# A head reordered: squares before copies, masks and keys on another engine, both bias halves in a row

## The chip, the core and the metric

The kernel runs on one core of a Trainium2 chip. Five engines work side by side, each through its own queue in order: TensorE (PE, matmuls and transposes), VectorE (DVE), ScalarE (ACT), GpSimd (POOL) and SyncE (SP, which here only issues DMAs). They wait for one another by semaphores. The metric is the device time of one launch in microseconds (us); lower is better.

## What is computed

Four images of 64 channels and 32x32 positions go through a local attention with windows of 7x7 (`conv`) and then through a token model whose steps are chosen by the data (`ffn`). The head of the kernel is the channel norm, the query fold and the position biases of the local attention:

```python
def _ln_c(v, eps=1e-06):
    m = jnp.mean(v, axis=1, keepdims=True)
    s = jnp.var(v, axis=1, keepdims=True)
    return (v - m) / jnp.sqrt(s + eps)
...
    q, k, v = (jnp.einsum('oc,bchw->bohw', w, xp) for w in (wq, wk, wv))   # xp: padded norm
    bias_x = jnp.einsum('bgxhw,xk->bhwk', qx, rel_x)       # qx, qy: halves of each group of q
    bias_y = jnp.einsum('bgyhw,yk->bhwk', qy, rel_y)
    logits = jnp.einsum('bchw,bchwkl->bhwkl', win_q, win_k)
    logits = logits + bias_x[:, :, :, None, :] + bias_y[:, :, :, :, None]
    attn = softmax(logits over the 49 window places)
    out = jnp.einsum('bhwkl,bchwkl->bchw', attn, win_v)
...
x = x + _L0_conv_ref(_ln_c(x), ...)
t = tokens(x);  t = t + _L0_ffn_ref(_ln_t(t), ...)
```

## The kernel before, in words

Two images lie on 128 partitions (64 channels each), so there are two image pairs, and each pair has 1024 positions in two chunks of 512: chunks 0 and 1 are "image 0" of the change's name, chunks 2 and 3 are "image 1". Each engine's program is written out by hand; its order is the order of the code, and nothing rearranges it.

The head runs from the loads to `scores(0)`. For each chunk j:

- TensorE: `centre(j)` (L346) subtracts the channel mean by a matmul into PSUM bank j.
- ScalarE: `square(0, j)` squares it into `sq` (L789) and copies it out to `xc` (L791).
- TensorE: `variance(0, j)` (L356) averages the squares with weights of 32 columns, four matmuls.
- ScalarE: `root(0, j)` (L806) takes the square root of variance plus epsilon.
- VectorE: `inverse(0, j)` (L1089) is its reciprocal.
- TensorE: `spread(0, j)` (L369) spreads it over the channels, four matmuls; it takes the whole width of the array.
- VectorE: `scale(0, j)` (L1106) multiplies `xc` by it into the padded image `h_pad` and raises `normed`.

Beside this chain TensorE turns the key weights and folds them with the query weights (`tables`, L387 and L389, and `fold_keys`, L396); ScalarE copies the results (`wk_nat` L820, `tabs` L825, `wqk_bd` L827). `queries(0)` (L404) makes the queries of chunk 0. `biases(a, half)` (L425, L428) makes half of the position biases of image pair a in 32 small matmuls, each 32 columns wide in the array. For each half, `add_bias` on VectorE (L1124, L1129) adds the masks and writes two operands of the scores. ScalarE writes the masks (L836, four copies of 32 rows, broadcast) and the keys' one-hot rows (L840, two instructions).

A matmul of float32 shows as two records in the trace: centre is x2, variance and spread are x8.

`scores(0)` (L471, L476) waits for the keys, the query copy and all four add_bias instructions. Then a loop over 16 pairs of blocks follows (scores, maxima, exponentials, normalise, transposes, mix), then the token model. Three more biases and later norms of the second kind use the same helpers in the loop.

Which PSUM bank holds what is set by tables: `QBANK` (queries), `BBANK` (biases), `CENTRE_AT`, `VAR_AT`, `SPREAD_AT`. The tables of `tables` and `fold_keys` lie in bank 7.

Of the kernel before, what the change touches and what calls it, by code (L numbers as in the profile page):

```python
# [25 lines left out]
ALU = mybir.AluOpType  # L26
# [3 lines left out]
P = 128  # L30
# [18 lines left out]
SCALE = float(C) ** -0.5  # L49
LN_C_EPS, LN_T_EPS = 1e-6, 1e-5  # L50
GBANK = (2, 6, 6, 6)
QBANK, VBANK, BBANK = (0, 7, 7, 7), (6, 7, 7, 7), (2, 3, 7, 7)
W2COLS = 2 * C + 2 + 1
TWICE = ((0, 0), (1, 0), (0, 1), (1, 1))
RING = 15
# [6 lines left out]
def build(nc, x, w_qk, w_q, w_v, bias_tables, key_onehot, masks, ident, mean_mat, spread_mat, iotas,  # L62
          attn_mask, ffn_mask, attn_pack, ffn_w1, ffn_pack, out):
    with ExitStack() as ctx:
# [278 lines left out]
        def _(pe):  # L343
            def centre(j, bank=None):

                nc.tensor.matmul(ps[:, j if bank is None else bank, :], centre_w[:], x2f[:, j * 512:j * 512 + 512],  # L346
                                 start=True, stop=True).then_inc(S["centred"], 1)

            def variance(k, j):

                bank, at = VAR_AT[k][j]
                pe.wait_ge(S["squared"], 4 * k + j + 1)
                if k == 0 and j >= 2:
                    pe.wait_ge(S["normed"], j - 1)
                for s in range(4):
                    mm = nc.tensor.matmul(ps[32 * s:32 * s + 32, bank, at:at + P], mean_w[:, P:P + 32],  # L356
                                          sq[:, j * 512 + P * s:j * 512 + P * s + P], start=True, stop=True)
                mm.then_inc(S["var_ready"], 1)

            def spread(k, j):  # L360

                banks, at = SPREAD_AT[k][j]
                if k == 1 and j < 3:
                    pe.wait_ge(S["rooted"], 1)
                else:
                    pe.wait_ge(S["inv_ready"], 5 if k else j + 1)
                for odd in range(2):
                    for r in range(2):
                        mm = nc.tensor.matmul(ps[:, banks[r], at + P * odd:at + P * odd + P],  # L369
                                              spread_w[C * r:C * r + C, odd, :],  # L370
                                              sq[C * r:C * r + C, j * 512:j * 512 + P], start=True, stop=True)
                mm.then_inc(S["spread_ready"], 1)
# [10 lines left out]
            def tables():  # L383

                pe.wait_ge(S["t_loaded"], 48)
                pe.wait_ge(S["eye_loaded"], 16)
                nc.tensor.transpose(ps[0:C, 5, 0:C], wqk[:, C:P], eye[0:C, 0:C]).then_inc(S["wk_turned"], 1)  # L387
                for h in range(2):
                    nc.tensor.matmul(ps[C * h:C * h + C, 7, 0:TX + TY], wq_nat[:], rel_tab[:],  # L389
                                     start=True, stop=True)  # L390

            def fold_keys():

                pe.wait_ge(S["wk_copied"], 1)
                for h in range(2):
                    mm = nc.tensor.matmul(ps[C * h:C * h + C, 7, P:P + C], wq_nat[:], wk_nat[:],  # L396
                                          start=True, stop=True)
                mm.then_inc(S["tab_ready"], 1)

# [35 lines left out]
            pe.wait_ge(S["x0_loaded"], 32)  # L435
            centre(0)
            centre(1)
            tables()
            variance(0, 0)
            fold_keys()  # L440
            pe.wait_ge(S["x1_loaded"], 32)
            centre(2)
            variance(0, 1)
            pe.wait_ge(S["s_loaded"], 64)
            spread(0, 0)
            pe.wait_ge(S["tab_copied"], 4)
            spread(0, 1)
            centre(3)
            variance(0, 2)
            pe.wait_ge(S["centre_copied"], 1)  # L450
            queries(0)
            pe.wait_ge(S["centre_copied"], 3)
            biases(0, 0)
            variance(0, 3)
            spread(0, 2)
            pe.wait_ge(S["centre_copied"], 4)
            biases(0, 1)
            spread(0, 3)

            def turn_row(bank, src=h2):  # L460
# [3 lines left out]
            def scores(p):  # L464

                a, hb, xb = p // 8, p % 8 // 2, p % 2
                blk = 4 * xb + hb
                if p >= 2:
                    pe.wait_ge(S["exp_done"], p - 1)
                for h in range(2):  # L470
                    nc.tensor.matmul(ps[:, 2 * xb + h, 0:NKEY], q_blk[C * h:C * h + C, a, blk, :],  # L471
                                     h_pad[C * h:C * h + C, a, BR * hb:BR * hb + KR, BC * xb:BC * xb + KC],
                                     start=True, stop=False)
                for part in range(2):
                    for h in range(2):
                        mm = nc.tensor.matmul(ps[:, 2 * xb + h, 0:NKEY], b_st[C * h:C * h + C, part, a, blk, :],  # L476
                                              k_st[C * h:C * h + C, part], start=False, stop=(part == 1))
                mm.then_inc(S["scores_ready"], 1)
# [38 lines left out]
            pe.wait_ge(S["q_copied"], 1)  # L517
            pe.wait_ge(S["bias_added"], 4)
            scores(0)
            scores(1)  # L520
            pe.wait_ge(S["w_loaded"], 32)
            pe.wait_ge(S["normed"], 4)
# [258 lines left out]
        def _(act):  # L781
# [2 lines left out]
                nc.scalar.activation(spare[:, 0:1], eps_c[:, 0:1], func)  # L784

            def square(k, j):
                bank = CENTRE_AT[k][j]
                act.wait_ge(S["centred"], 4 * k + j + 1)
                nc.scalar.activation(sq[:, j * 512:j * 512 + 512], ps[:, bank, :],  # L789
                                     ACT.Square).then_inc(S["squared"], 1)  # L790
                nc.scalar.copy(xc[:, j * 512:j * 512 + 512], ps[:, bank, :]).then_inc(S["centre_copied"], 1)  # L791

            def copy_variance(j):
                act.wait_ge(S["var_ready"], 4 + j + 1)
# [8 lines left out]
            def root(k, j):  # L803
                bank, at = VAR_AT[k][j]
                act.wait_ge(S["var_ready"], 4 * k + j + 1)
                nc.scalar.activation(sq[:, j * 512:j * 512 + P], ps[:, bank, at:at + P], ACT.Sqrt,  # L806
                                     bias=eps_c[:, k:k + 1]).then_inc(S["std_ready"], 1)
# [7 lines left out]
            act.wait_ge(S["eps_set"], 1)  # L815
            load_table(ACT.Sqrt)
            square(0, 0)
            act.wait_ge(S["w_zeroed"], 1)
            act.wait_ge(S["wk_turned"], 1)
            nc.scalar.copy(wk_nat[:], ps[0:C, 5, 0:C]).then_inc(S["wk_copied"], 1)  # L820
            square(0, 1)
            root(0, 0)
            act.wait_ge(S["tab_ready"], 1)
            for h in range(2):
                nc.scalar.copy(tabs[C * h:C * h + C, h, :], ps[C * h:C * h + C, 7, 0:TX + TY]  # L825
                               ).then_inc(S["tab_copied"], 1)
                nc.scalar.copy(wqk_bd[C * h:C * h + C, C * h:C * h + C], ps[C * h:C * h + C, 7, P:P + C]  # L827
                               ).then_inc(S["tab_copied"], 1)
            square(0, 2)
            root(0, 1)  # L830
            act.wait_ge(S["c_loaded"], 64)
            for h in range(2):
                for y in range(2):
                    rows = slice(C * h + 32 * y, C * h + 32 * y + 32)
                    src = masks_in[rows, 0:BR].unsqueeze(2) if y else masks_in[rows, 0:BC].unsqueeze(1)
                    nc.scalar.copy(masks_xy[rows, :].rearrange("p (r c) -> p r c", c=BC),  # L836
                                   src.broadcast_to([32, BR, BC])).then_inc(S["masks_set"], 1)
            act.wait_ge(S["k_loaded"], 32)
            for part in range(2):
                nc.scalar.mul(k_st[:, part], onehot[:, :, 0:KC], 1.0 - 2 * part).then_inc(S["keys_set"], 1)  # L840
            square(0, 3)
            root(0, 2)
            root(0, 3)
            load_table(ACT.Exp)

# [56 lines left out]
            for p in range(1, NPAIR - 2):  # L902
                copy_turned(p)
                copy_values(p + 1)
                if p in (3, 6):
                    copy_queries(2 + p // 6)
                if p in (4, 5):
                    copy_projected(p - 2)
                if p in (8, 10, 12):
                    square(1, p // 2 - 4)  # L910
                if p in (9, 11, 13):
                    copy_variance((p - 9) // 2)
                if p == 9:
                    load_next()
                exps(p + 2)
# [3 lines left out]
            root_three()  # L919
            copy_turned(15)  # L920
            square(1, 3)
            root(1, 3)
            load_table(ACT.Exp)

# [117 lines left out]
        def _(dve):  # L1042
# [71 lines left out]
            dve.wait_ge(S["pads_set"], 1)  # L1114
            scale(0, 0)
            scale(0, 1)
            inverse(0, 2)

            def add_bias(a, half):

# [9 lines left out]
                    b_map[:, 1, a, :, :, cols], b_top[:, 0, a, :, :, cols], -1e29, raw,  # L1130
                    ALU.max, ALU.subtract).then_inc(S["bias_added"], 1)

            dve.wait_ge(S["masks_set"], 4)
            add_bias(0, 0)
            inverse(0, 3)
            scale(0, 2)
            add_bias(0, 1)
            scale(0, 3)

            def maxima(p):  # L1140
# [292 lines left out]
```

## Time and profile before

| | us |
|---|---|
| median of 3 runs | 242.87 (242.84 to 243.87) |
| span of the profiled execution | 240.6 |
| TensorE matmul busy | 223.1 (93%) |
| VectorE busy | 157.0 (65%) |
| ScalarE busy | 158.3 (66%) |
| GpSimd busy | 26.2 (11%) |

The page gives the profiled execution's span, from its first instruction to its last, and no other time for it; the median of the runs is 2.27 above the span. Busy time is a sum over stages, and a busy TensorE is not one at its peak. What a change in the head is worth is read from the chain of waits and from the timelines of the engines in the first 24 us. A row of a timeline gives the start, the length from the first start to the last end of the instructions merged in it, and in brackets how long the engine was idle before it and what ended that.

### The profile page before, as it was taken

To read this page: it belongs to the slowest core of one execution; us is meant where nothing else is said; L and a number is where in the kernel's file an instruction comes from. 1 tells how busy PE (TensorE), PEld (TensorE's weight loads), DVE (VectorE), ACT (ScalarE), POOL (GpSimd) and SP (SyncE) were. 2 spreads that over 40 slices of the span, in tenths; PEclk is the share of its full clock that TensorE was granted. 3 is DMA by queue.
4 is the path that set the end of the run, shared out by engine and by line. 5 is a ranking of instruction groups with operands and counts; after the bars stand their busy time and mean duration, and the time that the engine had idled before them with its cause. 6 is when DMAs were issued, how large, how long until landed. Compare 5 with 4: busy or idle time off the path is not lost.

```text
span 240.6 us, 5412 instructions
## 1 busy us (share of the span) xinstructions
PE 223.1 (93%) x1995; PEld 153.9 (64%) x1996; DVE 157.0 (65%) x288; ACT 158.3 (66%) x310; POOL 26.2 (11%) x37
## 2 busy tenths in 40 slices
PE   7978989999899988999999999999999999998991
PEld 3347667666676665433576777888888888885320
DVE  1147636676866663664769999897679778753642
ACT  2573653476778784654579978789877777772641
POOL 9600231111212106200000000000000000000000
PEclk9999999999999999999999999999999999999998
DMA  6600000000010000000100000000000000000016
GB/s 141 149 0 5 0 1 4 3 0 0 4 33 3 1 3 0 0 4 11 34 0 4 0 3 0 3 1 3 0 3 0 3 0 1 3 3 0 0 29 147
DMA packets 3151, 3.60 MB, mean 15 GB/s; under 512 B 1077, under 2 KB 2229, under 8 KB 3126
## 3 DMA queue, kind: packets, MB, share of 16 engines
q1 hardware_dynamic: 2486, 2.59, 4.9%
q10 hardware_dynamic: 544, 0.66, 1.1%
q8 instruction: 16, 0.26, 0.4%
q14 instruction: 9, 0.07, 0.1%
q0 software_dynamic: 96, 0.00, 0.0%
HBM read 2.21 MB, written 1.05 MB: 14 GB/s over the span
## 4 chain that ended last, share of the span: by engine, by line
PE 74%; ACT 11%; DVE 9%; issue 5%; DVEq 0%; ACTq 0%
PE ps L681 12%; PE ps L667 11%; PE ps L646 11%; PE ps L734 6%; PE ps L748 6%; PE ps L509 4%; PE ps L497 3%; PE ps L471 3%; PE ps L381 3%; DVE negmax L1143 2%; ACT prob L866 2%; PE ps L346 2%; PE ps L627 1%; PE ps L425 1%; PE ps L486 1%
## 5 line engine op out<-in xcount | busy, mean ns | idle before, releaser
L1001 ACT COPY arena<-ps 128x1024 f32<-128x1024 f32 x32 | 32.4, 1012 | 15.8 <-PE ps L667 15.7
L646 PE MATMUL ps<-h_st,g_st 128*128 128x512 f32 x128 | 38.7, 424 | 0.7 <-ACT late L949 0.4
L1240 DVE TENSOR_REDUCE negmax<-ps 128x1 f32<-128x1024 f32 x32 | 38.4, 1217 | 1.4 <-PE ps L646 1.3
L949 ACT ACTIVATE late<-ps,negmax 128x1024 f32<-128x1024 f32 x32 | 35.9, 1122 | 5.0 <-DVE negmax L1240 4.4
L667 PE MATMUL ps<-eye,late 128*128 128x128 f32 x256 | 33.5, 274 | 0.6 <-DVE late L1250 0.2
L667 PEld LDWEIGHTS ps<-eye,late 128*128 128x128 f32 x256 | 29.1, 140 | 6.9 <-DVE late L1250 2.7
L681 PE MATMUL ps<-arena,late 128*64 128x128 f32 x512 | 31.5, 276 | 1.1 <-ACT arena L1001 1.1
L866 ACT ACTIVATE prob<-ps,negmax 128x308 f32<-128x308 f32 x32 | 16.4, 517 | 22.4 <-DVE negmax L1143 22.4
L681 PEld LDWEIGHTS ps<-arena,late 128*64 128x64 f32 x512 | 27.6, 137 | 3.8 <-issue 2.2
L646 PEld LDWEIGHTS ps<-h_st,g_st 128*128 128x128 f32 x128 | 21.8, 188 | 8.9 <-issue 3.2
L1250 DVE TENSOR_SCALAR late<-late,rinv 128x1024 f32<-128x1024 f32 x32 | 24.1, 754 | 1.1
L325 POOL TENSOR_TENSOR v_st<-arena,ones_c 128x308 f32<-128x308 f32 x16 | 11.9, 747 | 59.2 <-PE ps L486 37.9
L509 PE MATMUL ps<-prob_t,v_key 103*64 103x128 f32 x192 | 14.0, 281 | 4.5 <-ACT arena L856 1.1
L1143 DVE TENSOR_REDUCE negmax<-ps 128x2 f32<-128x616 f32 x16 | 12.7, 796 | 6.9 <-PE ps L476 6.9
L1016 ACT ACTIVATE arena<-ps,w2p 128x512 f32<-128x512 f32 x16 | 11.0, 690 | 7.1 <-PE ps L734 7.1
L734 PE MATMUL ps<-h,w1d 64*128 64x512 f32 x64 | 15.5, 614 | 0.0
L1152 DVE TENSOR_SCALAR prob<-prob,rinv 128x308 f32<-128x308 f32 x32 | 14.9, 507 | 0.6
L509 PEld LDWEIGHTS ps<-prob_t,v_key 103*64 103x64 f32 x192 | 10.2, 136 | 7.8 <-ACT arena L856 1.7
L748 PE MATMUL ps<-arena,w2p 128*64 128x512 f32 x64 | 15.1, 602 | 0.0
L877 ACT COPY prob_t<-ps 103x384 f32<-103x384 f32 x32 | 13.7, 485 | 1.6 <-PE ps L497 1.4
L497 PE MATMUL ps<-eye,prob 128*103 128x128 f32 x96 | 14.4, 286 | 0.2 <-DVE prob L1152 0.2
L1247 DVE RECIPROCAL rinv<-rowsum 128x1 f32<-128x1 f32 x32 | 5.1, 161 | 13.2 <-ACT late L949 12.3
(125 smaller groups left out, 317.7 us busy)
## 6 DMA issues: line engine op xcount, KB each, us to landing
out<-osum SPq DMA_DIRECT2D x8, 128.0 KB, 2.4
x<-in_x SPq DMA_DIRECT2D x2, 256.0 KB, 5.4
x<-in_x ACTq DMA_DIRECT2D x2, 256.0 KB, 5.9
onehot<-in_key_onehot SPq DMA_DIRECT2D x2, 133.0 KB, 2.8
w1d<-in_ffn_w SPq DMA_DIRECT2D x4, 64.0 KB, 2.2
w2p<-in_ffn_pack SPq DMA_DIRECT2D x2, 65.5 KB, 2.1
spread_w<-in_spread_mat SPq DMA_DIRECT2D x4, 32.0 KB, 5.8
mean_w<-in_mean_mat SPq DMA_DIRECT2D x1, 96.0 KB, 2.3
```

The costliest lines, as they stand in the source:

```text
L497: mm = nc.tensor.transpose(ps[0:CH, 4 + h, c * P:c * P + P], prob[:, pp, h, c * CH:c * CH + CH], eye[:])
L509: mm = nc.tensor.matmul(ps[C * h:C * h + C, 7, 0:P], v_key[0:CH, pp, c, C * h:C * h + C], prob_t[0:CH, pp, h, c, :], start=(c == 0), stop= ...
L646: mm = nc.tensor.matmul(ps[:, 2 * h + c, :], g_st[:, b2, h, q0:q0 + P], h_st[:, b2, h, part, c * 512:c * 512 + 512], start=(part == 0), st ...
L667: mm = nc.tensor.transpose(ps[:, bank + i, (c % 4) * P:(c % 4) * P + P], pr[:, n % 2, c * P:c * P + P], eye[:])
L681: mm = nc.tensor.matmul(ps[C * h:C * h + C, 7, cols], vk[:, g // 2, c, C * h:C * h + C], prt[:, g % 2, h, c, cols], start=(c == 0), stop=( ...
L734: mm = nc.tensor.matmul(ps[:, set0 + 2 * h + c, :], w1d[C * h:C * h + C, c * P:c * P + P], h2[C * h:C * h + C, t * 512:t * 512 + 512], sta ...
L748: mm = nc.tensor.matmul(ps[C * h:C * h + C, set0 + bank, :], w2p[:, c * C:c * C + C], hid[t % 2][:, 2 * h + c, :], start=(i == 0), stop=(i ...
L866: ins = nc.scalar.activation(prob[:, pp, h, 0:NKEY], ps[:, 2 * pp + h, 0:NKEY], ACT.Exp, bias=negmax[:, pp, h:h + 1], accum_out=rowsum[:, ...
L949: nc.scalar.activation(pr[:, n % 2, :], ps[:, 2 * (n % 2):2 * (n % 2) + 2, :], ACT.Exp, bias=negmax[:, 0, n % 2:n % 2 + 1], accum_out=rows ...
L1001: nc.scalar.copy(prt[:, n // 8 % 2, n % 2, :, q0:q0 + P], ps[:, bank:bank + 2, :].rearrange("p b (c q) -> p (b c) q", c=4)).then_inc(S["s_ ...
L1240: nc.vector.tensor_reduce(negmax[:, 0, n % 2:n % 2 + 1], ps[:, 2 * (n % 2):2 * (n % 2) + 2, :], mybir.AxisListType.XY, ALU.max, negate=Tru ...
L1250: nc.vector.tensor_scalar(pr[:, n % 2, :], pr[:, n % 2, :], rinv[:, 0, n % 2:n % 2 + 1], None, ALU.mult).then_inc(S["s_prob"], 1)
```

## The change

Four things are changed in the head, and the banks that go with them:

1. ScalarE's `square` is split into `square` and `copy_centred`. In the head both squares of image pair 0 stand ahead of their copies, the roots go between, and TensorE's `variance(0, 0)` and `variance(0, 1)` stand ahead of `tables` and `fold_keys`. The same split in the later loop keeps the order.
2. The masks and the keys are written by VectorE instead of ScalarE, behind `scale(0, 1)`.
3. TensorE centres chunk 3 and takes both variances of image pair 1 ahead of the biases; VectorE takes both its reciprocals ahead of the first `add_bias`.
4. Both bias halves stand in a row on TensorE, `queries(0)` and the two spreads of image pair 1 behind them; both `add_bias` stand in a row on VectorE, the two scales behind them.

The tables move to bank 3, the biases to banks 0 and 1, the first queries to bank 2. The wait for `tab_copied` now stands ahead of `centre(3)`, and `scores(1)` gets a wait for the last copy.

```diff
-QBANK, VBANK, BBANK = (0, 7, 7, 7), (6, 7, 7, 7), (2, 3, 7, 7)
+QBANK, VBANK, BBANK = (2, 7, 7, 7), (6, 7, 7, 7), (0, 1, 7, 7)
...
-                    nc.tensor.matmul(ps[C * h:C * h + C, 7, 0:TX + TY], wq_nat[:], rel_tab[:],
+                    nc.tensor.matmul(ps[C * h:C * h + C, 3, 0:TX + TY], wq_nat[:], rel_tab[:],
...
             centre(1)
+            variance(0, 0)
             tables()
-            variance(0, 0)
+            variance(0, 1)
             fold_keys()
             pe.wait_ge(S["x1_loaded"], 32)
             centre(2)
-            variance(0, 1)
             pe.wait_ge(S["s_loaded"], 64)
             spread(0, 0)
+            spread(0, 1)
             pe.wait_ge(S["tab_copied"], 4)
-            spread(0, 1)
             centre(3)
             variance(0, 2)
-            pe.wait_ge(S["centre_copied"], 1)
+            variance(0, 3)
+            biases(0, 0)
+            biases(0, 1)
+            pe.wait_ge(S["centre_copied"], 3)
             queries(0)
-            pe.wait_ge(S["centre_copied"], 3)
-            biases(0, 0)
-            variance(0, 3)
             spread(0, 2)
-            pe.wait_ge(S["centre_copied"], 4)
-            biases(0, 1)
             spread(0, 3)
...
             scores(0)
+            pe.wait_ge(S["centre_copied"], 4)
             scores(1)
...
             square(0, 0)
+            square(0, 1)
+            root(0, 0)
             act.wait_ge(S["w_zeroed"], 1)
             act.wait_ge(S["wk_turned"], 1)
             nc.scalar.copy(wk_nat[:], ps[0:C, 5, 0:C]).then_inc(S["wk_copied"], 1)
-            square(0, 1)
-            root(0, 0)
+            copy_centred(0, 0)
+            root(0, 1)
+            copy_centred(0, 1)
...
             square(0, 2)
-            root(0, 1)
-            act.wait_ge(S["c_loaded"], 64)
...
-                    nc.scalar.copy(masks_xy[rows, :].rearrange("p (r c) -> p r c", c=BC),
...
-            act.wait_ge(S["k_loaded"], 32)
...
-                nc.scalar.mul(k_st[:, part], onehot[:, :, 0:KC], 1.0 - 2 * part).then_inc(S["keys_set"], 1)
+            copy_centred(0, 2)
             square(0, 3)
             root(0, 2)
+            copy_centred(0, 3)
             root(0, 3)
...
             scale(0, 0)
             scale(0, 1)
-            inverse(0, 2)
...
+            dve.wait_ge(S["c_loaded"], 64)
+            for h in range(2):
+                for y in range(2):
+                    rows = slice(C * h + 32 * y, C * h + 32 * y + 32)
+                    src = masks_in[rows, 0:BR].unsqueeze(2) if y else masks_in[rows, 0:BC].unsqueeze(1)
+                    nc.vector.tensor_copy(masks_xy[rows, :].rearrange("p (r c) -> p r c", c=BC),
+                                          src.broadcast_to([32, BR, BC])).then_inc(S["masks_set"], 1)
+            dve.wait_ge(S["k_loaded"], 32)
+            for part in range(2):
+                nc.vector.tensor_scalar(k_st[:, part], onehot[:, :, 0:KC], 1.0 - 2 * part, None, ALU.mult
+                                        ).then_inc(S["keys_set"], 1)
+            inverse(0, 2)
+            inverse(0, 3)
             dve.wait_ge(S["masks_set"], 4)
             add_bias(0, 0)
-            inverse(0, 3)
+            add_bias(0, 1)
             scale(0, 2)
-            add_bias(0, 1)
             scale(0, 3)
```

ScalarE before, from the first copy of a chunk to the root of chunk 1 (the last row; ps is PSUM, sq the squares and later the roots, xc the centred chunk):

```order
L791 COPY xc<-ps 128x512
L820 COPY wk_nat<-ps 64x64 [waits wk_turned,w_zeroed]
L789 ACTIVATE sq<-ps 128x512 [waits centred]
L791 COPY xc<-ps 128x512
L806 ACTIVATE sq<-ps,eps_c 128x128 [waits var_ready]
L825 COPY tabs<-ps 64x98 [waits tab_ready]
L827 COPY wqk_bd<-ps 64x64
L825 COPY tabs<-ps 64x98
L827 COPY wqk_bd<-ps 64x64
L789 ACTIVATE sq<-ps 128x512 [waits centred]
L791 COPY xc<-ps 128x512
L806 ACTIVATE sq<-ps,eps_c 128x128 [waits var_ready]
```

ScalarE in the changed kernel, from the squares of chunks 0 and 1 (the first row is both) to the table copies:

```order
L787 ACTIVATE sq<-ps 128x512 [waits centred] x2
L808 ACTIVATE sq<-ps,eps_c 128x128 [waits var_ready]
L824 COPY wk_nat<-ps 64x64 [waits wk_turned,w_zeroed]
L792 COPY xc<-ps 128x512 [waits centred]
L808 ACTIVATE sq<-ps,eps_c 128x128 [waits var_ready]
L792 COPY xc<-ps 128x512 [waits centred]
L830 COPY tabs<-ps 64x98 [waits tab_ready]
L832 COPY wqk_bd<-ps 64x64
```

The root of chunk 1 has moved from behind four table copies, a square and three chunk copies to behind one chunk copy.

VectorE before, from the scale of chunk 1 to that of chunk 3 (h_st holds the scores' bias operands and the keys, late holds the padded image):

```order
L1106 TENSOR_TENSOR late<-xc,ps 128x16x32 [waits spread_ready,centre_copied]
L1089 RECIPROCAL sq<-sq 128x128 [waits std_ready]
L1124 TENSOR_TENSOR h_st<-ps,masks_xy 128x64x8 [waits bias_ready,masks_set]
L1129 SCALAR_TENSOR_TENSOR h_st<-h_st,ps 128x64x8 [waits bias_added]
L1089 RECIPROCAL sq<-sq 128x128 [waits std_ready]
L1106 TENSOR_TENSOR late<-xc,ps 128x16x32 [waits spread_ready,centre_copied]
L1124 TENSOR_TENSOR h_st<-ps,masks_xy 128x64x8 [waits bias_ready]
L1129 SCALAR_TENSOR_TENSOR h_st<-h_st,ps 128x64x8 [waits bias_added]
L1106 TENSOR_TENSOR late<-xc,ps 128x16x32 [waits spread_ready,centre_copied]
```

VectorE in the changed kernel, the same stretch:

```order
L1104 TENSOR_TENSOR late<-xc,ps 128x16x32 [waits spread_ready,centre_copied]
L1135 COPY masks_xy<-masks_in 32x128 [waits c_loaded]
L1135 COPY masks_xy<-masks_in 32x128 x3
L1139 TENSOR_SCALAR h_st<-onehot 128x308 [waits k_loaded]
L1139 TENSOR_SCALAR h_st<-onehot 128x308
L1087 RECIPROCAL sq<-sq 128x128 [waits std_ready] x2
L1121 TENSOR_TENSOR h_st<-ps,masks_xy 128x64x8 [waits bias_ready,masks_set]
L1126 SCALAR_TENSOR_TENSOR h_st<-h_st,ps 128x64x8 [waits bias_added]
L1121 TENSOR_TENSOR h_st<-ps,masks_xy 128x64x8 [waits bias_ready]
L1126 SCALAR_TENSOR_TENSOR h_st<-h_st,ps 128x64x8 [waits bias_added]
L1104 TENSOR_TENSOR late<-xc,ps 128x16x32 [waits spread_ready,centre_copied] x2
```

Six mask and key instructions have come in, and both add_bias now stand behind both reciprocals and ahead of both scales.

## Rows read from the trace of the kernel before

**Rows 1.** The page, part 4: the chain that ended last, by engine.

```profile
PE 74%; ACT 11%; DVE 9%; issue 5%; DVEq 0%; ACTq 0%
```

**Rows 2.** The chain of waits, 8 to 24 us: start, us, what.

```profile
13.07 0.96 DVE sq L1089
...
14.17 0.71 PE ps L369 x8
...
19.51 0.70 DVE h_st L1124
...
22.33 0.68 DVE h_st L1124
...
23.03 0.70 DVE h_st L1129
```

**Rows 3.** Timeline of ScalarE, 8 to 15 us: start, us, engine, line, operation.

```profile
8.46 0.60 ACT L789 ACTIVATE sq<-ps 128x512 f32<-128x512 f32 x1 [2.33 <-PE ps L346]
8.96 0.58 ACT L791 COPY xc<-ps 128x512 f32<-128x512 f32 x1
...
10.96 0.23 ACT L825 COPY tabs<-ps 64x98 f32<-64x98 f32 x1
...
11.70 0.60 ACT L789 ACTIVATE sq<-ps 128x512 f32<-128x512 f32 x1
...
12.65 0.39 ACT L806 ACTIVATE sq<-ps,eps_c 128x128 f32<-128x128 f32 x1
12.92 1.24 ACT L836 COPY masks_xy<-masks_in 32x128 f32<-32x128 f32 x4
14.18 0.82 ACT L840 ACTIVATE h_st<-onehot 128x308 fp32r<-128x308 f32 x2
```

**Rows 4.** Timeline of TensorE, 7 to 11 us.

```profile
7.40 1.88 PE L346 MATMUL ps<-x,centre_w 128*128 128x512 f32 x4
...
9.29 0.24 PE L387 MATMUL ps<-eye,wqk 64*64 64x64 f32 x1
...
9.78 0.43 PE L356 MATMUL ps<-sq,mean_w 128*32 128x128 f32 x8
...
10.13 0.33 PE L396 MATMUL ps<-wk_nat,wq_nat 64*64 64x64 f32 x4
...
10.40 1.12 PE L346 MATMUL ps<-x,centre_w 128*128 128x512 f32 x2
```

**Rows 5.** Timeline of TensorE, 14 to 24 us; of each bias block the first row.

```profile
14.82 1.12 PE L346 MATMUL ps<-x,centre_w 128*128 128x512 f32 x2
15.87 0.43 PE L356 MATMUL ps<-sq,mean_w 128*32 128x128 f32 x8
16.23 1.16 PE L404 MATMUL ps<-late,wqk_bd 128*128 128x512 f32 x2
17.32 0.28 PE L425 MATMUL ps<-late,tabs 128*32 128x64 f32 x1
...
20.17 0.29 PE L425 MATMUL ps<-late,tabs 128*32 128x64 f32 x1
...
22.14 0.71 PE L369 MATMUL ps<-sq,spread_w 64*128 64x128 f32 x8
23.86 0.76 PE L471 MATMUL ps<-late,arena 64*128 64x308 f32 x3 [1.00 <-DVE h_st L1129]
```

**Rows 6.** VectorE: a group of instructions (busy, mean ns), and timelines at 27 and 64 us.

```profile
L1152 DVE TENSOR_SCALAR prob<-prob,rinv 128x308 f32<-128x308 f32 x32 | 14.9, 507 | 0.6
...
27.22 0.67 DVE L1152 TENSOR_SCALAR prob<-prob,rinv 128x308 f32<-128x308 f32 x2
...
64.31 0.28 DVE L1204 COPY twice_w<-eye 64x64 f32<-64x64 f32 x2
...
64.41 0.38 DVE L1204 COPY twice_w<-eye 64x64 f32<-64x64 f32 x2
```

**Rows 7.** Busy time in 13 to 14 us: PE, PEld, DVE, ACT, POOL, granted clock, DMA.

```profile
13.00:14.00 1.00, 0.00 (x0) 0.00 (x0) 0.93 (x2) 0.93 (x5) 0.00 (x0) 1.00 0.00 0
```

More of the change, by code:

```diff
@@ L395, in fold_keys @@
                 for h in range(2):
-                    mm = nc.tensor.matmul(ps[C * h:C * h + C, 7, P:P + C], wq_nat[:], wk_nat[:],
+                    mm = nc.tensor.matmul(ps[C * h:C * h + C, 3, P:P + C], wq_nat[:], wk_nat[:],
                                           start=True, stop=True)
@@ L786, in square, with copy_centred @@
             def square(k, j):
-                bank = CENTRE_AT[k][j]
                 act.wait_ge(S["centred"], 4 * k + j + 1)
-                nc.scalar.activation(sq[:, j * 512:j * 512 + 512], ps[:, bank, :],
+                nc.scalar.activation(sq[:, j * 512:j * 512 + 512], ps[:, CENTRE_AT[k][j], :],
                                      ACT.Square).then_inc(S["squared"], 1)
-                nc.scalar.copy(xc[:, j * 512:j * 512 + 512], ps[:, bank, :]).then_inc(S["centre_copied"], 1)
+            def copy_centred(k, j):
+                act.wait_ge(S["centred"], 4 * k + j + 1)
+                nc.scalar.copy(xc[:, j * 512:j * 512 + 512], ps[:, CENTRE_AT[k][j], :]
+                               ).then_inc(S["centre_copied"], 1)
             def copy_variance(j):
@@ L820, in _ @@
             nc.scalar.copy(wk_nat[:], ps[0:C, 5, 0:C]).then_inc(S["wk_copied"], 1)
-            square(0, 1)
-            root(0, 0)
+            copy_centred(0, 0)
+            root(0, 1)
+            copy_centred(0, 1)
             act.wait_ge(S["tab_ready"], 1)
             for h in range(2):
-                nc.scalar.copy(tabs[C * h:C * h + C, h, :], ps[C * h:C * h + C, 7, 0:TX + TY]
+                nc.scalar.copy(tabs[C * h:C * h + C, h, :], ps[C * h:C * h + C, 3, 0:TX + TY]
                                ).then_inc(S["tab_copied"], 1)
-                nc.scalar.copy(wqk_bd[C * h:C * h + C, C * h:C * h + C], ps[C * h:C * h + C, 7, P:P + C]
+                nc.scalar.copy(wqk_bd[C * h:C * h + C, C * h:C * h + C], ps[C * h:C * h + C, 3, P:P + C]
                                ).then_inc(S["tab_copied"], 1)
             square(0, 2)
-            root(0, 1)
-            act.wait_ge(S["c_loaded"], 64)
[L832 to L835, printed above, removed]
-                    nc.scalar.copy(masks_xy[rows, :].rearrange("p (r c) -> p r c", c=BC),
-                                   src.broadcast_to([32, BR, BC])).then_inc(S["masks_set"], 1)
-            act.wait_ge(S["k_loaded"], 32)
-            for part in range(2):
-                nc.scalar.mul(k_st[:, part], onehot[:, :, 0:KC], 1.0 - 2 * part).then_inc(S["keys_set"], 1)
+            copy_centred(0, 2)
             square(0, 3)
             root(0, 2)
+            copy_centred(0, 3)
             root(0, 3)
@@ L910, in _ @@
                     square(1, p // 2 - 4)
+                    copy_centred(1, p // 2 - 4)
                 if p in (9, 11, 13):
@@ L921, in _ @@
             square(1, 3)
+            copy_centred(1, 3)
             root(1, 3)
```

## The prediction

> **What bounds the kernel now.** I read the page's chain of waits first: most of the span is TensorE [rows 1], so the program is one long chain and there is no slack at its end for work that starts late. The change touches the first 24 us alone, so I then followed the chain from 8 us to the first scores. Three things are to be seen there. First, ScalarE copies chunks (xc, the first at 8.96) that nobody needs yet, and its roots stand behind: the root of chunk 1 starts at 12.65 [rows 3]. So VectorE's reciprocal of chunk 1 starts only at 13.07, TensorE is idle until its spread at 14.17, and centre(3) starts at 14.82 [rows 2, 5]. Second, from there TensorE works without a break through centre(3), a variance, queries(0), the two halves of the bias and the rest, until 22.8 or so [rows 5]. Third, VectorE ends the head: reciprocal and scale stand ahead of the second add_bias, whose two instructions run from 22.33 to 23.73, and scores(0) starts at 23.86 after 1.00 us of idle TensorE [rows 2, 5]. After that the loop over pairs has the same instructions in the same order in both kernels, and all its waits are on work of its own; the last DMA of the head (onehot) has long been used [rows 3]. So what scores(0) gains, the end gains. **The price of the change is the start of scores(0), against 23.86.**
>
> **Part 1: roots ahead of copies (image pair 0).** I walk the new order with the durations of now; a "slot" is the distance to the next start on the same engine. square(0,0) starts at 8.46 as now; a square or a copy has a slot of 0.50 (8.46 to 8.96) [rows 3]. centre(1) ends at 9.28 [rows 4], so square(0,1) runs 9.32 to 9.92. variance(0,0), now ahead of the tables, starts when centre(1) hands over, where the tables start now (9.29), and lasts 0.43 [rows 4]: 9.30 to 9.73. So root(0,0) takes ScalarE's next slot at 9.82 and its 0.39 ends at about 10.2 [rows 3]; the reciprocal (0.96) runs 10.23 to 11.18 [rows 2]. TensorE meanwhile does the tables from 9.66 (slot 0.49, from 9.29 to 9.78) and variance(0,1) from 10.15 to 10.58 [rows 4]. ScalarE does the small copy wk_nat at 10.10 (0.1 to 0.2) and one xc copy (0.50), and starts root(0,1) at 10.71, where it now starts at 12.65 [rows 3]. The second reciprocal then runs 11.12 to 12.07 instead of from 13.07 [rows 2].
>
> That is 1.95 us earlier, but TensorE cannot use it all: fold_keys at 10.51 (0.27), centre(2) at 10.78 (slot 1.05, as 14.82 to 15.87), spread(0,0) at 11.83 and spread(0,1) at 12.48 (slot 0.65, as 14.17 to 14.82) put centre(3) at 13.13 [rows 2, 4, 5]. The two spreads no longer wait. **Gain so far 14.82 - 13.13 = 1.69 us.** The wait of centre(3) for tab_copied is new (the tables now lie in bank 3, which centre(3) overwrites): ScalarE has one xc copy and the four table copies (10.96 to 11.70 now, 0.74) behind root(0,1), so it is done at 12.3 and the wait is covered by 0.9 [rows 3].
>
> **Part 2: both bias halves in a row.** From centre(3) TensorE has: centre(3) 1.05; variance(0,2) 0.36 (15.87 to 16.23), whose square is long done; a wait for square(0,3), since centre(3) ends at 14.25, the square 0.60 later, and variance(0,3) starts at 14.97: 0.43 of idle; variance(0,3) 0.36; two bias blocks; queries(0) 1.09 (16.23 to 17.32); two spreads, 0.65 each [rows 3, 5]. One block lasts 1.97 up to an instruction that takes the whole array (20.17 to 22.14), which includes a wait for a reciprocal; the sequence 17.32 to 20.17 less a variance (0.36) and a spread (0.65) leaves 1.84 for the other [rows 5]. I take 3.7 for the two, with 3.5 to 3.9 for the range. Sum 1.05 + 0.36 + 0.43 + 0.36 + 3.7 + 1.09 + 1.30 = 8.29; now it is 23.86 - 14.82 = 9.04. **Gain of this part 0.75 us**: the 1.00 of idle ahead of scores(0) goes, and about 0.4 of new wait comes. scores(0) would start at 13.13 + 8.29 = 21.42, if VectorE and ScalarE are ready by then.
>
> **Part 3: masks and keys on VectorE.** This takes 1.24 + 0.82 us from ScalarE [rows 3]. It is needed there: ScalarE is done with chunk 2 at about 13.2, and with 2.06 more it would come to square(0,3) at 15.3, not at 14.29, which Part 2 takes; those 1.0 us are in its sum. On VectorE they stand behind scale(0,1), which waits for spread(0,1) and ends at 14.65, and ahead of the two reciprocals; behind those stand both add_bias, for which scores(0) waits. The trace has no mask or key instruction on VectorE. Bounds: a mask copy 0.19 (64 columns on VectorE, 0.38 / 2) [rows 6] to 0.31 (ScalarE's own 1.24 / 4) [rows 3]; a key 0.34 (0.67 / 2) to 0.51 (the mean of all 32), both 128x308 TENSOR_SCALAR [rows 6]. I take 0.29 and 0.35, near ScalarE's copy since the masks have 128 columns: 1.16 + 0.70 = 1.9, from 14.55 to 16.45. The two reciprocals (0.96 each at most) end by 18.4, or 18.2 where the second starts before the first has quite ended [rows 2]. The first half of the bias is there 2.19 after its block starts (17.32 to 19.51): 15.33 + 2.19 = 17.5 [rows 2, 5], so the first add_bias goes at 18.1, VectorE-bound, and takes 1.40 (22.33 to 23.73); the second starts at 19.5, since its half is there at about 19.3, and ends at 20.9; 0.13 more to TensorE (23.73 to 23.86) is 21.0. **So TensorE sets scores(0) at 21.42, with VectorE 0.4 behind it as a near second.** queries(0) ends at 20.2 and its copy at 20.8, 0.6 ahead. scale(0,2) and scale(0,3) come last now and end at about 22.2; the first maxima starts 1.1 after scores(0), at 22.5, so they are hidden by 0.3.
>
> Of the four L1204 copies, which are alike, the first two, in the same rows, together take 0.28, the second and third, where the rows change from 0 to 64, 0.38: a step to other rows takes away the overlap [rows 6]. The Trainium skill's page "VectorE: DVE Perf Modes", section "Two Vector instructions with no wait between them", states that an instruction whose operand starts in another quarter of the partitions is held until the earlier ones have finished. The row agrees. Each mask copy starts in another quarter, so by the rule the four don't overlap (1.16 as I took it); with 0.08 to 0.1 of overlap, as between the first two, they would take some 0.9, and VectorE would be ready at 20.7 instead of 21.0. The sum is the same by both; the cover left is 0.4 by the rule, 0.7 without.
>
> The other edits cost nothing: the banks are exchanged one for one, squares and copies of image pair 1 keep their order, and scores(1)'s new wait is for a copy that ends at about 15.5.
>
> **Sum.** 1.69 + 0.75 = 2.44 us. The profiled execution has a span of 240.6 and should have 238.2; the page gives no other time for it. The median of the runs is 242.87, that is 2.27 outside the span, which I leave as it is: 242.87 - 2.44 = **240.4 us**.
>
> **Rivals.**
> *VectorE becomes the bound.* If masks, keys or reciprocals take 1.2 us more than my 1.9 (six instructions at 0.52 each, the slowest key price), 0.8 of it shows: 241.2. At twice what I took, 3.8, 1.5 of it shows and the time is 241.9: no change that can be told. Against it: nothing else moves data beside VectorE there. For it: the cover is only 0.4.
> *Part of the gain is eaten on TensorE.* Bias blocks at 1.97 each and slower hand-overs cost 0.3 to 0.9: 240.8 to 241.4. The 0.43 of new wait for square(0,3) is the place: it grows if ScalarE is late with what stands ahead.
> *More gain.* Blocks at 1.75 each and centre slots of 0.94 (half of the two back to back, 1.88) [rows 4] instead of 1.05 give 0.4 more, to where VectorE binds at 21.0: 240.0; with masks and keys at their lower prices (4 x 0.19 + 2 x 0.34 = 1.4) up to 239.5.
> *The granted clock falls.* Slower than before needs this: if TensorE's clock fell to 1.2 GHz in the new wait at 14.5, the 6.5 us of matmuls up to scores(0) would double, and the time would be 240.4 + 6.5 = 246.9; from 2.44 us of doubled work on the kernel is slower. Against it: the stretch of now with no matmul at all, 13 to 14 us, shows 1.00 granted, 2.4 GHz [rows 7], and the new order has shorter gaps. The Trainium skill's page "TensorE: Matmul & The Clock Gate", section "What's actually happening", states that the clock is gated by how busy the array was; this trace shows no fall in the head.
> *The change does nothing.* This would need the loop to wait for something not in the head; the trace shows none.
>
> **How the numbers follow.** A measurement of this kernel can tell about 0.5%, 1.2 us. Forecast as summed, 240.0 to 241.0: 0.66. Gain partly eaten on TensorE or by VectorE, 241.0 to 241.6: 0.12. More gain, 239.4 to 240.0: 0.10. VectorE so slow, or the loop so bound, that nothing is seen (241.7 to 244): 0.08. Clock or something like it, slower: 0.04. Faster 0.88, same 0.08, slower 0.04. The range takes in the first three but for their far ends: 239.5 to 241.6.
>
> **What would show it.** In the profile of the changed kernel: the second reciprocal at about 11.1 and centre(3) at 13.1 with no idle TensorE between spreads (Part 1); two bias blocks without a variance between them, in 3.7 us, and scores(0) at 21.4, released by TensorE's own queue (Part 2); six mask and key instructions in 1.9 us and the last add_bias at 20.9 (Part 3); after scores(0) the same distances as before. If scores(0) shows a wait for bias_added, Part 3 is under-priced; if centre(3) is not earlier than 13.5, Part 1 is wrong; if scores(0) is at 21.4 and the time has not moved, the claim that the gain reaches the end is wrong.

## The result, and the profile after

The changed kernel took 239.31 us in the median of 4 runs (239.01 to 239.68), against 242.86 for the kernel before; the ratio is 0.9846 (95% interval 0.9819 to 0.9873). So it is faster by 3.55 us or 1.5%, where 2.44 us were forecast, and the time lies 0.19 us below the range. Run again later it took 239.75 against 242.79, a ratio of 0.9876 (0.9859 to 0.9894): 3.04 us, inside the range. The sign and the mechanism held; the size of the gain was too small in the forecast both times.

The page of the changed kernel has a span of 237.2 us, 3.4 below that of before. Its chain, which answers to [rows 1], has less of ScalarE and VectorE in it and more of TensorE:

```profile
PE 77%; ACT 10%; DVE 7%; issue 5%; DVEq 0%; ACTq 0%
```

TensorE's timeline in the head of the changed kernel, in answer to [rows 4, 5]:

```profile
7.08 1.96 PE L346 MATMUL ps<-x,centre_w 128*128 128x512 f32 x4
...
11.48 1.16 PE L369 MATMUL ps<-sq,spread_w 64*128 64x128 f32 x16
12.57 1.12 PE L346 MATMUL ps<-x,centre_w 128*128 128x512 f32 x2
13.63 0.43 PE L356 MATMUL ps<-sq,mean_w 128*32 128x128 f32 x8
14.38 0.43 PE L356 MATMUL ps<-sq,mean_w 128*32 128x128 f32 x8 [0.33 <-ACT sq L787]
...
14.62 0.28 PE L425 MATMUL ps<-late,tabs 128*32 128x64 f32 x1
...
18.50 1.16 PE L404 MATMUL ps<-late,wqk_bd 128*128 128x512 f32 x2
19.59 1.16 PE L369 MATMUL ps<-sq,spread_w 64*128 64x128 f32 x16
20.59 0.69 PE L469 MATMUL ps<-late,arena 64*128 64x308 f32 x4
```

Three idle stretches of before are gone: 1.00 us ahead of scores(0) at 23.86 [rows 5], and two ahead of the spreads of image pair 0, which the timeline of the kernel before shows so:

```profile
12.19 0.71 PE L369 MATMUL ps<-sq,spread_w 64*128 64x128 f32 x8 [0.32 <-DVE sq L1089]
14.17 0.71 PE L369 MATMUL ps<-sq,spread_w 64*128 64x128 f32 x8 [1.26 <-DVE sq L1089]
```

One idle stretch is new, 0.33 us ahead of the variance of chunk 3, which waits for its square. So idle time fell by 2.25 us (0.32 + 1.26 + 1.00 less 0.33); what else the head gained is TensorE's own work taking less time in the new order. Both pairs of spreads now merge into one row of x16, and scores(0) (L469 here) starts at 20.59 with no wait ahead of it.

VectorE in the changed kernel: both reciprocals of image pair 0 in one row, four masks, two keys, the next two reciprocals, then the two add_bias:

```profile
9.95 1.78 DVE L1087 RECIPROCAL sq<-sq 128x128 f32<-128x128 f32 x2 [6.33 <-ACT sq L808]
...
13.54 0.96 DVE L1135 COPY masks_xy<-masks_in 32x128 f32<-32x128 f32 x4
14.53 0.55 DVE L1139 TENSOR_SCALAR h_st<-onehot 128x308 fp32r<-128x308 f32 x2
15.00 1.75 DVE L1087 RECIPROCAL sq<-sq 128x128 f32<-128x128 f32 x2
...
18.65 0.69 DVE L1121 TENSOR_TENSOR h_st<-ps,masks_xy 128x512 fp32r<-128x512 f32 x1 [0.40 <-PE ps L428]
19.38 0.69 DVE L1126 SCALAR_TENSOR_TENSOR h_st<-h_st,ps 128x512 fp32r<-128x512 f32 x1
20.42 0.69 DVE L1104 TENSOR_TENSOR late<-xc,ps 128x512 f32<-128x512 f32 x1 [0.35 <-PE ps L369]
```

Before the second add_bias VectorE now waits 0.40 us for TensorE; in the kernel before it was TensorE that waited for VectorE [rows 2, 5].

### The profile page after: what moved, and what is told of

Its sections match the earlier page's. It is cut to its first block, busy times and chain, and to the rows that moved or that the text cites. A ratio compares the mean times of both kernels' runs of the same rounds, so it can differ in the third digit from the quotient of the medians.

```text
span 237.2 us, 5409 instructions
## 1 busy us (share of the span) xinstructions
PE 222.1 (94%) x1995; PEld 153.4 (65%) x1996; DVE 158.4 (67%) x294; ACT 156.1 (66%) x304; POOL 26.2 (11%) x37
## 4 chain that ended last, share of the span: by engine, by line
PE 77%; ACT 10%; DVE 7%; issue 5%; DVEq 0%; ACTq 0%
PE ps L680 12%; PE ps L666 12%; PE ps L645 12%; PE ps L733 6%; PE ps L747 6%; PE ps L507 4%; PE ps L495 4%; PE ps L469 3%; PE ps L381 2%; DVE negmax L1152 2%; ACT prob L862 2%; PE ps L346 2%; PE ps L425 2%; PE ps L369 2%; PE ps L626 2%
```

## The experiments

Two theories were set against each other for the 1.1 us that the forecast lacked. **N (neighbours):** a short TensorE block costs less beside its like than the distance I had read off for it. **S (start):** the first real matmul, centre(0), starts at a time that differs from run to run, 7.40 us in the profile of before and 7.08 in that of the changed kernel. To keep the two apart, this table gives for each profile the start of centre(0), that of scores(0) and their distance, which the start cannot touch but for 0.08 us: the row of centre(0) and centre(1) lasts 1.88 where it came straight behind the idle matmuls (both profiles of before, masks on ScalarE, and the first two of variance between) and 1.95 or 1.96 in the others.

| kernel | centre(0) | scores(0) | distance | median us | ratio to before (95%) |
|---|---|---|---|---|---|
| before | 7.40 | 23.86 | 16.46 | 242.86 | |
| before, again | 7.41 | 23.78 | 16.37 | 242.88 | 1.0019 (0.9999 to 1.004) |
| changed | 7.08 | 20.59 | 13.51 | 239.31 | 0.9846 (0.9819 to 0.9873) |
| changed, again | 7.55 | 21.04 | 13.49 | 239.75 | 0.9876 (0.9859 to 0.9894) |
| Part 1 alone | 7.23 | 21.77 | 14.54 | 240.61 | 0.9923 (0.9908 to 0.9939) |
| masks on ScalarE | 8.05 | 22.51 | 14.46 | 240.76 | 0.9918 (0.9902 to 0.9935) |
| old tail | 7.44 | 21.98 | 14.54 | 240.80 | 0.9923 (0.9903 to 0.9942) |
| spreads doubled | 6.89 | 21.25 | 14.36 | 240.64 | 0.9919 (0.9900 to 0.9938) |
| VectorE loaded | 7.37 | 21.64 | 14.27 | 240.77 | 0.9918 (0.9896 to 0.9939) |
| variance between | 6.96 | 19.82 | 12.86 | 238.99 | 0.9865 (0.9841 to 0.9889) |
| variance between, again | 7.88 | 20.76 | 12.88 | 239.09 | 0.9842 (0.9815 to 0.9869) |
| the same, three idle matmuls | 7.07 | 20.02 | 12.95 | 238.71 | 0.9823 (0.9796 to 0.9849) |

**Both kernels again.** No edit.

> The kernel before, unchanged, for its spread and for where its first real matmul starts. The changed kernel gained 3.55 us where 2.44 were forecast. Theory N (neighbours): TensorE's short blocks cost less next to their like than I took, some 0.8 us of the difference; then before stays at 242.8, with centre(0) starting between 7.0 and 7.5 us depending on when the clock rises. Rival S (start): part of the difference is the start of the first matmul, 7.40 in the one profile and 7.08 in the other, which is a matter of the run; then this kernel's runs scatter by 0.3 to 0.6 us with the granted clock (0.995 to 1.000).

> The changed kernel, unchanged. By theory N the difference to before at equal granted clock is 3.0 to 3.3 us; by rival S alone it is 2.4 to 2.7 at equal clock, and the 3.55 was luck. Its runs so far show 236.9 and 237.2 us of span at clock 1.000 and 237.6 at 0.995, so some 0.3 to 0.6 us belongs to the start in any case.

The distances repeat within 0.1 us: 16.46 and 16.37 before, 13.51 and 13.49 after. So the head is shorter by 2.9 us, 0.5 more than forecast. The rest is S: in the profiles of all kernels, which share everything up to centre(0), that matmul starts anywhere from 6.89 to 8.05. The two profiles of the changed kernel show it: one span is 0.5 us longer (237.7 against 237.2), and its centre(0) starts 0.47 later. Of the 3.55 us of the first comparison about 0.6 was thus the scatter of the runs; the other half of the miss is N's, which the doubled spreads below show. The times alone would not have told it: the runs at a granted clock of 0.999 or 1.000 are 242.2 to 242.6 before and 239.4 to 239.9 in the changed kernel when both were run again, some 2.7 us apart, which the expectation gave to S (2.4 to 2.7) and not to N (3.0 to 3.3).

**Part 1 alone.** The squares, roots and variances of image pair 0 as in the changed kernel; the masks and keys on ScalarE, ahead of the square of chunk 3; the tail of TensorE and VectorE as before.

```diff
 (against the changed kernel, ScalarE)
             copy_centred(0, 2)
+            act.wait_ge(S["c_loaded"], 64)      # four mask copies and two keys, as before
...
             square(0, 3)
 (TensorE)
             variance(0, 2)
+            pe.wait_ge(S["centre_copied"], 3)
+            queries(0)
+            biases(0, 0)
             variance(0, 3)
-            biases(0, 0)
+            spread(0, 2)
             biases(0, 1)
-            pe.wait_ge(S["centre_copied"], 3)
-            queries(0)
-            spread(0, 2)
             spread(0, 3)
 (VectorE: masks and keys gone)
             inverse(0, 2)
-            inverse(0, 3)
             add_bias(0, 0)
+            inverse(0, 3)
+            scale(0, 2)
             add_bias(0, 1)
-            scale(0, 2)
             scale(0, 3)
```

> Part 1 alone: squares, roots and variances of chunks 0 and 1 as in the changed kernel; masks and keys still on ScalarE (ahead of the square of chunk 3), biases, queries and reciprocals in the old order. By the prediction's own Part 1 (1.69 us) it would be at 241.2. Theory N: the two spreads in a row are 0.2 shorter than taken and centre(3) starts near 12.6, and the rest of the head shrinks a little as VectorE comes sooner to the last add_bias: scores(0) at 21.6 to 21.9, 240.6 to 240.9. Rival: Part 1 is worth nothing by itself, because VectorE still ends the head: within 0.5 of before.

It took 240.61 us; the distance fell from 16.4 to 14.54, by 1.9. The forecast's Part 1 was 1.69, and the 0.2 more is the pair of spreads ahead of centre(3): 1.10 us (11.63 to 12.73) where 1.30 had been taken. The wait for VectorE at the end of the head is still there, as long as before [rows 5]; all of it was merely moved. TensorE's timeline of this kernel:

```profile
21.77 0.76 PE L469 MATMUL ps<-late,arena 64*128 64x308 f32 x3 [0.99 <-DVE h_st L1136]
```

**Masks and keys on ScalarE again**, everything else as in the changed kernel.

```diff
 (ScalarE)
             copy_centred(0, 2)
+            act.wait_ge(S["c_loaded"], 64)
...
+            act.wait_ge(S["k_loaded"], 32)
...
             square(0, 3)
 (VectorE)
-            dve.wait_ge(S["c_loaded"], 64)
...
-            dve.wait_ge(S["k_loaded"], 32)
...
             inverse(0, 2)
```

> The changed kernel with one part undone: masks and keys are written by ScalarE again, ahead of the square of chunk 3. The prediction puts 1.0 us on this. Theory N, from the changed kernel's trace: ScalarE is free at 12.86, 2.06 us of masks and keys push the square of chunk 3 from 13.73 to 14.9 and the variance and both bias blocks with it: scores(0) 1.1 to 1.2 later than 20.59, 240.4 to 240.6. Rival: the move to VectorE was not needed, since the biases have slack: same as the changed kernel, 239.3.

240.76 us, 1.0 above the changed kernel run beside it, and 0.96 in the distance. ScalarE's timeline shows why: masks and keys stand ahead of the square of chunk 3, which is late, and TensorE waits for it 1.39 us instead of 0.33.

```profile
13.72 1.25 ACT L841 COPY masks_xy<-masks_in 32x128 f32<-32x128 f32 x4
14.99 0.82 ACT L845 ACTIVATE h_st<-onehot 128x308 fp32r<-128x308 f32 x2
15.71 0.57 ACT L787 ACTIVATE sq<-ps 128x512 f32<-128x512 f32 x1
```

```profile
16.34 0.43 PE L356 MATMUL ps<-sq,mean_w 128*32 128x128 f32 x8 [1.39 <-ACT sq L787]
```

**Part 2 undone**, masks and keys on VectorE: the tail of TensorE and VectorE as in the diff of Part 1 alone, with ScalarE as in the changed kernel.

> The changed kernel with the two bias halves apart again (queries ahead of them, a variance and a spread between, a reciprocal and a scale between the two add_bias), masks and keys still on VectorE. This is Part 2 undone. The prediction's Part 2 gives 0.75 us: 240.1. Theory N: two spreads apart cost 0.4 to 0.5 more than in a row, and VectorE again ends the head with reciprocal, scale and add_bias: scores(0) at 21.5 to 21.7, 240.2 to 240.4. Rival: the order of the tail does not matter once masks and keys are off ScalarE: 239.3 to 239.6.

240.80 us, and a distance of 14.54, the very one of Part 1 alone. So the move of the masks by itself brings nothing, and the new tail with the masks on ScalarE next to nothing (14.46): together they bring 1.04. The time is 0.4 above what was expected, since centre(0) of this profile started 0.36 later than that of the changed kernel; with that taken off, scores(0) is at 21.62, as expected. With the old tail VectorE's row of reciprocal, scale and add_bias ends the head whoever writes the masks; with the new tail the square of chunk 3 is on the path, and ScalarE must be free for it. VectorE's end of the head here, and TensorE's wait for it:

```profile
18.97 0.95 DVE L1087 RECIPROCAL sq<-sq 128x128 f32<-128x128 f32 x1
19.83 0.63 DVE L1104 TENSOR_TENSOR late<-xc,ps 128x512 f32<-128x512 f32 x1
20.42 0.69 DVE L1121 TENSOR_TENSOR h_st<-ps,masks_xy 128x512 fp32r<-128x512 f32 x1
21.15 0.69 DVE L1126 SCALAR_TENSOR_TENSOR h_st<-h_st,ps 128x512 fp32r<-128x512 f32 x1
```

```profile
21.98 0.76 PE L469 MATMUL ps<-late,arena 64*128 64x308 f32 x3 [0.98 <-DVE h_st L1126]
```

**The spreads doubled**: the disputed price by itself.

```diff
             queries(0)
+            (the wait and the four matmuls of spread(0, 2), same place, raising nothing)
             spread(0, 2)
+            (the wait and the four matmuls of spread(0, 3), same place, raising nothing)
             spread(0, 3)
```

> The disputed cost by itself: the changed kernel with each of the last two spreads issued twice, so four spreads stand in a row ahead of scores(0); the doubles write the same values to the same place. I priced a spread at 0.65. Theory N: one next to its like costs 0.43 to 0.46, so scores(0) moves by 0.86 to 0.92 and the time is 240.2. Rival (0.65 each is right and the short tail came from elsewhere): 1.30 later, 240.6.

240.64 us; the distance grew by 0.86 for two spreads, 0.43 each. The time by itself is the one that the rival named; it is 1.33 above the first median of the changed kernel, but 0.89 above the later one (239.75), so here the distance decides and not the time. TensorE's timeline shows the slots: 0.54 for the first, which stands behind queries(0), then 0.45, 0.45 and 0.44 up to scores(0), never 0.65.

```profile
19.37 0.72 PE L459 MATMUL ps<-sq,spread_w 64*128 64x128 f32 x8
19.91 0.61 PE L369 MATMUL ps<-sq,spread_w 64*128 64x128 f32 x8
20.36 0.61 PE L466 MATMUL ps<-sq,spread_w 64*128 64x128 f32 x8
20.81 0.61 PE L369 MATMUL ps<-sq,spread_w 64*128 64x128 f32 x8
21.25 0.69 PE L481 MATMUL ps<-late,arena 64*128 64x308 f32 x4
```

**VectorE loaded**: eight more mask copies ahead of the real ones, written into osum, which is overwritten later.

```diff
             dve.wait_ge(S["c_loaded"], 64)
+            for again in range(2):
...
+                        nc.vector.tensor_copy(osum[rows, P * again:P * again + P]..., src...)
```

> The cover of Part 3: the changed kernel with eight more mask copies on VectorE ahead of the real ones (written where nothing is read before it is written over), some 1.9 us at 0.24 each. The changed kernel's trace shows VectorE idle for 0.09 ahead of the first add_bias, 0.40 ahead of the second, and done 0.39 ahead of scores(0) where it needs 0.13 of hand-over within that: 0.9 of cover. So scores(0) moves by 1.0, 240.3. Rival (VectorE already sets scores(0)): the whole 1.9, 241.2. Rival (VectorE does not matter here): 239.3.

The eight copies took 1.84 us and the distance grew by 0.77, so VectorE had some 1.1 us of cover in the changed kernel. Now it does set scores(0). VectorE's row of the copies and TensorE's wait:

```profile
13.83 1.84 DVE L1136 COPY osum<-masks_in 32x128 f32<-32x128 f32 x8
```

```profile
21.64 0.76 PE L469 MATMUL ps<-late,arena 64*128 64x308 f32 x3 [0.60 <-DVE h_st L1126]
```

**The variance between the bias halves**: a version to beat both.

```diff
 (TensorE)
             variance(0, 2)
-            variance(0, 3)
             biases(0, 0)
+            variance(0, 3)
             biases(0, 1)
 (VectorE)
             inverse(0, 2)
-            inverse(0, 3)
             add_bias(0, 0)
+            inverse(0, 3)
             add_bias(0, 1)
```

> A version that may beat both: the first bias half starts right behind the variance of chunk 2, while ScalarE squares chunk 3; the variance of chunk 3 stands between the halves, its reciprocal between the two add_bias. If, as theory N says, a variance (32 columns wide) costs only 0.24 next to a bias and the one idle stretch left on TensorE (0.33 us ahead of the variance of chunk 3) is on the path, scores(0) starts 0.4 to 0.5 sooner, near 20.1, and the time is 238.8 to 238.9. Rival: VectorE is the near second that the prediction named; then its reciprocal ahead of the second add_bias takes the gain, and the time stays at 239.2 to 239.4.

238.99 us, ratio 0.9865 (0.9841 to 0.9889), and 239.09 when run once more; the distance is 12.86 and 12.88, some 0.64 less than in the changed kernel, of which 0.08 is the shorter row of centre(0). The wait of 0.33 is gone, since the first bias block now fills it; the rest is the two variances taking less time beside the biases. VectorE no longer waits for TensorE ahead of the second add_bias, but TensorE doesn't wait for it either, so the two are about level. TensorE's first bias row and scores(0), then VectorE:

```profile
13.68 0.28 PE L425 MATMUL ps<-late,tabs 128*32 128x64 f32 x1
...
19.82 0.69 PE L469 MATMUL ps<-late,arena 64*128 64x308 f32 x4
```

```profile
17.21 0.95 DVE L1087 RECIPROCAL sq<-sq 128x128 f32<-128x128 f32 x1
18.07 0.63 DVE L1121 TENSOR_TENSOR h_st<-ps,masks_xy 128x512 fp32r<-128x512 f32 x1
18.73 0.69 DVE L1126 SCALAR_TENSOR_TENSOR h_st<-h_st,ps 128x512 fp32r<-128x512 f32 x1
```

**The start**: that version again, and with three idle matmuls instead of four ahead of centre(0).

```diff
-            for i in range(4):
+            for i in range(3):
                 nc.tensor.matmul(ps[:, 6, :], idle_in[:, 0:P], idle_in[:], start=True, stop=True)
```

> The version with the variance of chunk 3 between the bias halves once more, to be compared with the next one on the same chip, and for a second start of the first matmul. From its first trace centre(0) to scores(0) takes 12.86 us against 13.50 in the changed kernel and 16.42 in the one before, so 0.64 less than the changed kernel: 238.9 to 239.1. If the traces' starts (6.89 to 8.05 so far, whatever the head) are luck, centre(0) starts somewhere else in that range and the distance to scores(0) is 12.86 again.

> The same with three instead of four idle matmuls ahead of the first real one. In five of ten traces the first real matmul waited for the images' DMA, 0.2 to 0.64 us after the last idle one; in the others it came straight behind the idle ones, which are slow until the clock rises. Theory S (the start is set by whichever is later, the idle matmuls or the DMA): 0 to 0.4 us sooner in the median, 238.6 to 239.0. Rival (fewer idle matmuls, later rise of the clock): the first real ones run at half clock, each chunk's centre takes 0.85 to 1.0 more, 239.5 to 240.5.

With four, the idle matmuls (L381) of this profile ran until 8.04, and centre(0) started at 7.88, straight behind them. With three they ended by 6.93 and centre(0) started at 7.07; its row is as long as in the changed kernel (1.96). First the version with four, then with three:

```profile
1.44 6.60 PE L381 MATMUL ps<-idle_in 128*128 128x512 f32 x8 [1.44 <-DVE idle_in L1041]
7.88 1.88 PE L346 MATMUL ps<-x,centre_w 128*128 128x512 f32 x4
```

```profile
1.44 5.49 PE L381 MATMUL ps<-idle_in 128*128 128x512 f32 x6 [1.44 <-DVE idle_in L1041]
7.07 1.96 PE L346 MATMUL ps<-x,centre_w 128*128 128x512 f32 x4
```

The medians are 239.09 and 238.71. The two sets of five runs overlap a little (238.73 to 239.59 and 238.24 to 238.88), so 0.4 us is likely and not certain. Other profiles show the second bound on the start, the images' DMA: in that of the old tail centre(0) waits for it.

```profile
7.44 1.96 PE L346 MATMUL ps<-x,centre_w 128*128 128x512 f32 x4 [0.60 <-DMA x<-in_x]
```

That fewer idle matmuls never slow the real ones is not shown: this is one profile and five runs.

## Where the prediction was right, and the step that failed

**What failed: the price of a spread (Parts 1 and 2).** The prediction read its slot as 0.65 from a single spread followed by centre(3) [rows 2, 5] and used it for all four. But a spread between its like costs 0.45, as the doubled spreads show directly, and one with its like on one side and a matmul over all 128 rows on the other about 0.54: the pair ahead of centre(3) took 1.09 (11.48 to 12.57; by the single records of the trace the second starts at 12.02), the pair ahead of scores(0) 1.00 (19.59 to 20.59). So 0.65 holds for a spread alone ahead of such a matmul, and the sum had 0.21 too much in Part 1 and 0.30 in Part 2, which is the whole 0.51 by which the forecast distance of 14.02 (7.40 to 21.42) missed 13.51. The experiments give the same by parts: Part 1 brought 1.9 for 1.69, the rest 1.04 for 0.75. Each spread alternates between the upper and the lower 64 rows. The Trainium skill's page "TensorE: Matmul & The Clock Gate", section "The mechanism" of its part on row and column tiling, states that weights load under running matmuls only where these use other rows; the cheap slot beside its like and the 0.1 more at a side where all 128 rows are in use fit that. No run separates this from another reason for that 0.1.

Two other slips in Part 2 nearly cancel. The two bias blocks took 3.88 (14.62 to 18.50), not 3.7: the prediction held that the 1.97 of one block included a wait for a reciprocal, but the row at 22.14 has no idle time ahead of it [rows 5] and the reciprocal (from 20.84) was done by 21.78. The variance ahead of them 0.24, not 0.36. The wait for the square of chunk 3 was there, 0.39 against 0.43.

**What the rest of the miss was.** The profile of the changed kernel started centre(0) 0.32 sooner than that of before; the stretch from scores(0) to the end was 216.6 against 216.7, and what lies outside the span 2.1 against 2.27. The 2.27 was a mis-sized term: it sets the median of the runs against the span of one of them, while every run on record takes 2.0 to 2.2 more than its own span. With 0.51 these make the 1.1 us between 240.4 and 239.31. None of them is the change's; the second comparison, with 3.04, has less of them. The 0.51 alone would have left the time at 239.9, inside the range, and the rest alone at 239.8; it took both to leave it. The range should have taken in some 0.3 us of such scatter on its low side, since the start of centre(0) hangs on the end of the idle matmuls and on a DMA, both of which the prediction had taken as fixed.

**The rival "more gain" was near in number and not in reason.** It named 239.5 to 240.0 for bias blocks at 1.75, centre slots of 0.94 and cheap masks and keys. The blocks took 1.94 each and centre(3) 1.06; masks and keys were cheap, but VectorE did not set the time.

**Right: Part 1's chain.** The second reciprocal came straight behind the first, TensorE did not wait between its spreads, and Part 1 alone gave 1.9 us where 1.69 were forecast.

**Right: the link of Part 2 and Part 3.** The claim that the masks on ScalarE would hold the square of chunk 3 by 1.0 us measured 0.96. That neither of the two parts brings anything without the other, the prediction did not say.

**Right in kind, too cautious in size: VectorE as near second.** Masks and keys took 1.46 us (13.54 to 15.00) instead of 1.9: 0.24 from one mask to the next, 0.55 for both keys. The cover was some 1.1 instead of 0.4, so this rival did not come. The cheaper masks and keys are 0.44 of that difference. Another 0.7 is a slip in the sum: it had scale(0,1) end at 14.65, but by the rows of before a scale starts 0.82 behind its spread (14.17 to 14.99) and takes 0.69, which from a spread at 12.48 gives 13.99. The scores, which came 0.5 sooner, took some back.

```profile
14.99 0.69 DVE L1106 TENSOR_TENSOR late<-xc,ps 128x512 f32<-128x512 f32 x1 [0.42 <-PE ps L369]
```

The mask copies indeed don't overlap: each lasts 0.22 and the four take 0.96.

**Right: the gain reaches the end.** From scores(0) to the end of the span it is 216.7 before and 216.6 after, and within 0.5 of that in every profile but one. The exception is the profile with the masks on ScalarE, 218.1, in which the granted clock fell to 0.76 and 0.67 between 88 and 94 us; the other runs of that kernel are 1.7 to 2.5 us shorter.

```profile
88.00:91.00 3.00, 2.40 (x22) 2.19 (x22) 0.69 (x2) 2.07 (x5) 0.00 (x0) 0.76 0.00 0
91.00:94.00 3.00, 3.00 (x25) 2.11 (x24) 1.58 (x4) 0.00 (x0) 2.49 (x2) 0.67 0.00 0
```

**The clock rival** did not come: the granted clock reads 1.00 all through the head of the changed kernel.

## What to carry to other kernels

Price a short matmul block by what stands next to it, not by one distance read off the trace: the same spread cost 0.45 us between its like, 0.54 at the end of a row of them and 0.65 alone ahead of a block over all rows, and an order that puts like beside like gains that difference by itself. When a head ends in two engines that wait for one another by turns, test the parts of a reorder in pairs: here each of two moves was worth nothing alone and 1.0 us with the other. And compare two kernels by the distance between two marks inside the head, since the start of the first matmul alone moved by over a microsecond from profile to profile.

## What the runs showed of the hardware

TensorE's first real matmul is bound by two things that differ from run to run: the idle matmuls, whose eight records took 5.2 to 6.8 us in the profiles, and the landing of the images, which was last in five of them. The single records of an idle matmul last 1.06 us at first and 0.59 later, and how many are long differs from profile to profile; the granted clock reads 1.00 in that stretch, so its rows do not say why. With one idle matmul fewer the first real ones were as long as before (1.96 in the one profile). A fall of the granted clock in mid-kernel (0.67 to 0.76 over 6 us) went with 1.5 us more from scores(0) to the end in one profile; no other profile shows one there.
